# Graph layer on one Trainium2 core: a comparison moved to ScalarE, four comparisons merged into one, six node units moved into hop 2, output steps begun at tick 33

## The reference

```python
h = relu(layernorm(x))
agg = segment_sum(relu(h[src]), dst)            # layer 0
x = x + relu(relu((h + agg) @ W1 + b1) @ W2 + b2)
h = relu(layernorm(x))                          # layer 1, 8 heads of 8
Q = relu(h @ Wq + bq); K = h @ Wk + bk; V = h @ Wv + bv
hidden = V * hopwise[0]
for hop in range(3):
    if hop == 0:
        Kj = relu(K[row] + ef)
        msg = norm * outer(Kj, V[row]);  M = segment_sum(msg, col)
    else:
        M = segment_sum(norm * M[row], col)
    H = einsum("nhi,nhij->nhj", Q, M)
    H = H / max(1, |H| / sqrt(8))
    hidden += hopwise[hop + 1] * H
x = x + hidden
```

## Time and profile before

| | us |
|---|---|
| median of 3 runs | 1729.83 (1729.37 to 1741.05) |
| the profiled execution | 1737.73, its span 1735.0 |
| source pass, gathers | 3.7 to 285 |
| destination pass, gathers | 286 to 594 |
| hop 0, gathers | 640 to 895 |
| hop 1, gathers | 933 to 1190 |
| hop 2, gathers | 1211 to 1471 |
| scatters of the output | 1472 to 1725 |

### The profile page before, as it was taken

One profiled execution on the slowest core, in us unless ns is written; L12 is line 12 of the kernel. 1 busy time (PEld: TensorE's weight loads), 2 busy tenths in 40 slices (PEclk: granted clock), 3 DMA queues, 4 the chain that ended last, 5 costly groups with the idle time before them and its releaser, 6 DMA issues. The chain is left out here.

```text
span 1735.0 us, 22194 instructions
## 1 busy us (share of the span) xinstructions
PE 1301.4 (75%) x5794; PEld 800.3 (46%) x5794; DVE 1487.6 (86%) x3207; ACT 1017.0 (59%) x2815; POOL 1203.7 (69%) x1185
## 2 busy tenths in 40 slices
PE   3788888878888858777771777776588999777771
PEld 2666666656555534554550333323233444454551
DVE  5999999979999958999997999996456788799991
ACT  4688887858999954554552455553455666333330
POOL 7777766707777517777744777774777777777776
PEclk9799999979999967988895899899799999988886
DMA  5255554425666547999995788886345545466640
GB/s 130 80 115 114 127 123 113 127 70 147 159 170 157 145 93 249 317 320 314 305 313 183 271 308 305 300 307 242 92 124 155 158 135 154 132 177 173 176 138 16
DMA packets 281219, 313.83 MB, mean 181 GB/s; under 512 B 169009, under 2 KB 198569, under 8 KB 268550
## 3 DMA queue, kind: packets, MB, share of 16 engines
q1 hardware_dynamic: 224166, 246.39, 45.8%
q0 software_dynamic: 56928, 66.04, 15.0%
HBM read 214.54 MB, written 161.32 MB: 217 GB/s over the span
## 5 line engine op out<-in xcount | busy, mean ns | idle before, releaser
L946 PE MATMUL bank<-product,ident 128*128 128x512 f32 (+1 forms) x800 | 382.5, 635 | 137.6 <-DVE product L1302 137.5
L549 POOL DMA_INDIRECT state<-state_hop,slot_of_src x392 | 395.2, 1008 | 126.1 <-issue 108.0
L719 ACT ACTIVATE bank<-state,norm 128x512 f32<-128x512 f32 x392 | 251.2, 679 | 254.2 <-DMA state<-state_hop,slot_of_src 218.0
L1302 DVE TENSOR_TENSOR product<-bank,queries 128x512 f32<-128x512 f32 x392 | 261.9, 689 | 91.3 <-ACT bank L719 89.6
L946 PEld LDWEIGHTS bank<-product,ident 128*128 128x128 f32 x800 | 160.6, 206 | 357.7 <-issue 183.7
L511 POOL DMA_INDIRECT x_edges<-in_x,dst_tiles x196 | 203.5, 1039 | 106.2 <-issue 53.9
L525 POOL DMA_INDIRECT row_of_src<-node_rows,pos_int x196 | 195.3, 996 | 104.1 <-issue 54.3
L511 POOL DMA_INDIRECT x_edges<-in_x,src_tiles x196 | 210.0, 1071 | 75.1 <-issue 55.2
L565 POOL DMA_INDIRECT out<-rows,dst_out x196 | 193.3, 986 | 59.7 <-issue 58.8
L1300 DVE SCALAR_TENSOR_TENSOR acc<-acc,same_as_before,bank 128x512 f32<-128x512 f32 x196 | 145.7, 744 | 15.1 <-ACT bank L719 14.7
L1113 DVE SCALAR_TENSOR_TENSOR acc<-acc,same_as_before,bank 128x512 f32<-128x512 f32 x196 | 145.8, 744 | 1.7
(11 more groups left out here) (220 smaller groups left out, 2992.1 us busy)
## 6 DMA issues: line engine op xcount, KB each, us to landing
state_hop<-acc SPq DMA_DIRECT2D x98, 1024.0 KB, 4.6
x_nodes<-in_x SPq DMA_DIRECT2D x49, 256.0 KB, 4.2
src_row<-in_src_row SPq DMA_DIRECT2D x49, 256.0 KB, 3.9
out<-out_rows SPq DMA_DIRECT2D x49, 256.0 KB
dst_row<-in_dst_row SPq DMA_DIRECT2D x49, 256.0 KB, 3.4
kv_rows<-kv SPq DMA_DIRECT2D x49, 256.0 KB, 3.1
gg<-head_sums SPq DMA_DIRECT2D x98, 128.0 KB
kv_back<-kv_rows SPq DMA_DIRECT2D x49, 256.0 KB
```

The lines of the kernel that those rows point to most:

```text
L549: pool.indirect_dma_start(out=mg[u % 4][:, k, :], out_offset=None, in_=d_m[hop - 1], in_offset=bass.IndirectOffsetOnAxis(ap=sidx[:, t:t + ...
L719: act.activation(pw[t % len(pw)][:, :], mg[u % 4][:, k, :], ACT.Copy, scale=wn12[:, t:t + 1]).then_inc(weighted, 1)
L946: ins = ten.matmul(ph[:, 0:k * D].rearrange("p (c j) -> p c j", j=HD), ident[:, :], part, start=(r == 0), stop=(r == HD - 1))
L1302: vec.tensor_tensor(ihj(pr[m % 2][:, u % 2 * EH + k, :]), ihj(pw[t % len(pw)][:, :]), over_j(Q[:, t, :]), ALU.mult).then_inc(multiplied, 1)
```

## The change

1. `gsel` is made by ScalarE: Sign of `src_row` minus the first destination plus a half (1 or -1), at the end of its tick. `delta` is halved, its last column and the first row are set so that the product gives the same count; for this one more load (15 instead of 14) and three small VectorE operations stand before the first tick.
2. The four 128x128 comparisons of a unit become one 128x512 comparison with a broadcast column, behind the statistics.
3. The last six node units leave ticks 82 to 97 and run at E0+4, E0+8, ... E0+24. There the third product shares bank 0 with the two turns (`value_bank`), so TensorE waits before a turn until the sum of the older unit has been read; SP's first load of them waits for hop 1's states.
4. The head sums of hop 2 come one tick later in TensorE's queue.
5. The output steps in hop 2 begin at the first fitting tick from E0+33 (E0+34) instead of E0+10. So three full steps (f = 0, 1, 2) instead of eleven come before tick E0+50, and the last step is at E0+100 instead of E0+92.

```diff
-for g in range(E0 + 10, E0 + 3 * CU):
+for g in range(E0 + 33, E0 + 3 * CU):
...
-DENSE_TICKS = DENSE_TICKS[0:DU]
+DE = DU - 6
+DENSE_TICKS = DENSE_TICKS[0:DE] + [E0 + 4 + 4 * k for k in range(DU - DE)]
...
+        rowb = sb("row_begins", [P, 1])
...
+        def value_bank(m):
+
+            return pvd if m < DE else ptd
...
-        N_LOADS = 14
+        N_LOADS = 15
...
                 wait(sync, x1_d, m - RX + 1)
+                if m == DE:
+                    sync.wait_ge(carried, 2)
+                    for b in range(3):
+                        sync.wait_ge(m1_kept[b], landed(CU - 1, b, 3))
...
+                u = g - 1
+                if 0 <= u < CU:
+                    if u == 0:
+                        act.wait_ge(consts_set, 1)
+                    act.wait_ge(srow_in[u % 3], landed(u, u % 3, 3))
+                    wait(act, searched, u - 1)
+                    act.activation(gsel[u % 2][:, :], srow[u % 3][:, :], ACT.Sign, bias=rowb[:, 0:1]).then_inc(g_set, 1)
...
-                    rows_out(pvd, hT2d, Wv, 1, HT // 2, mm3_d)
+                    rows_out(value_bank(m), hT2d, Wv, 1, HT // 2, mm3_d)
...
+                    if m >= DE:
+                        wait(ten, res_d, len([t for t in DENSE_TICKS if t + 7 <= g]))
...
-                    m = group_ready(u) if 0 <= u < CU else None
+                    v = u if hop == 1 else u - 1
+                    m = group_ready(v) if 0 <= v < CU else None
...
+            step(vec.tensor_scalar(dprev[0:1, :], dprev[0:1, :], -1.0, None, ALU.mult))
             step(vec.tensor_tensor(delta[:, 0:T], dpm[:, :], dprev[:, :], ALU.subtract))
+            own.add(vec.tensor_scalar(delta[:, 0:T], delta[:, 0:T], 0.5, None, ALU.mult))
+            own.add(vec.tensor_scalar(rowb[:, :], dpm[:, 0:1], -1.0, 0.5, ALU.mult, ALU.add))
...
-                            ins = vec.tensor_scalar(sel[u % 2][:, k * P:(k + 1) * P], drow[u % 3][:, k * P:(k + 1) * P],
-                                                    tmf[:, t:t + 1], None, ALU.is_equal)
...
-                u = g - 1
-                if 0 <= u < CU:
-                    vec.wait_ge(srow_in[u % 3], landed(u, u % 3, 3))
-                    wait(vec, searched, u - 1)
-                    vec.tensor_scalar(gsel[u % 2][:, :], srow[u % 3][:, :], dpm[:, 0:1], None, ALU.is_ge).then_inc(g_set, 1)
+                u = g - S0
+                if 0 <= u < AU:
+                    vec.wait_ge(drow_in[u % 3], landed(u, u % 3, 3))
+                    wait(vec, turned_e, u - 1)
+                    vec.tensor_tensor(sel[u % 2][:, :].rearrange("p (k c) -> p k c", c=P),
+                                      drow[u % 3][:, :].rearrange("p (k c) -> p k c", c=P),
+                                      tmf[:, u * EH:(u + 1) * EH].unsqueeze(2).to_broadcast([P, EH, P]),
+                                      ALU.is_equal).then_inc(s_set, 1)
```

More of the change, by code:

```diff
@@ L397, in _ @@
             for to, what in ((dpm[:, :], dst_pm), (dprev[1:P, :], dst_pm[0:P - 1, :]),
+                             (dprev[0:1, :], dst_pm[P - 1:P, :]),
                              (brow[:, :], biases.unsqueeze(0).to_broadcast([3, 4 * P])),
@@ L942, in _ @@
                         if hop == 2 and m == 0:
-                            ten.wait_ge(res_d, DU)
+                            ten.wait_ge(res_d, DE)
                         for r in range(HD):
@@ L1080, in _ @@
             own.add(vec.memset(ones3[:, :], 1.0))
-            own.add(vec.memset(dprev[0:1, :], 0.0))
-            own.add(vec.memset(delta[:, T:T + 1], float(T)))
+            step(vec.memset(delta[:, T:T + 1], T / 2))
+            own.add(vec.memset(delta[0:1, T:T + 1], T + (P - 1) * T / 2))
             own.sync()
@@ L1121, in _ @@
                 qp, q = st[(g - 1) % RS], st[g % RS]
-                n_sel = 0
-                def select(n):
-                    nonlocal n_sel
-                    u = g - S0
-                    if 0 <= u < AU:
-                        if n_sel == 0:
-                            vec.wait_ge(drow_in[u % 3], landed(u, u % 3, 3))
-                            wait(vec, turned_e, u - 1)
-                        for k in range(n_sel, n_sel + n):
-                            t = u * EH + k
-                            ins = vec.tensor_scalar(sel[u % 2][:, k * P:(k + 1) * P], drow[u % 3][:, k * P:(k + 1) * P],
-                                                    tmf[:, t:t + 1], None, ALU.is_equal)
-                        n_sel += n
-                        if n_sel == EH:
-                            ins.then_inc(s_set, 1)
                 if g - 1 in STAT_NO:
@@ L1143, in _ @@
                     own.add(vec.reciprocal(qp[:, 4, lo:hi], qp[:, 3, lo:hi]))
-                    select(1)
                     own.sync()
@@ L1153, in _ @@
                     wait(vec, out_kept[m % 2], landed(m - 2, m % 2, 2))
-                    vec.tensor_tensor(flat(rd[m % 2][:, :, :]), pvd[:, :], flat(x1d[m % R1][:, 0, :, :]), ALU.add).then_inc(res_d, 1)
+                    vec.tensor_tensor(flat(rd[m % 2][:, :, :]), value_bank(m)[:, :], flat(x1d[m % R1][:, 0, :, :]), ALU.add).then_inc(res_d, 1)
                 m = DENSE_AT.get(g - 4)
@@ L1234, in _ @@
                         vec.wait_ge(x1_kept[b], landed(AU - 1, b, 4))
-                    vec.wait_ge(res_d, DU)
+                    vec.wait_ge(res_d, DE)
                     own.add(vec.memset(accz[2][:, EH - 1, :], 0.0))
```

5 lines of the change are left out of this document (removed).

## The result

| | before | after |
|---|---|---|
| time, median (lowest to highest) | 1734.1 us (1729.4 to 1741.1) | 1809.4 us (1803.9 to 1813.5) |
| ratio, with its 95% interval | | 1.043 (1.038 to 1.048) |
| span of the profiled execution | 1735.0 us | 1811.6 us |
| granted clock of TensorE | 0.890 | 0.864 |

The account below looks back on a forecast made before the run. From 1211 us to the end one GpSimd queue was taken as the bound, and its gathers before. Terms +1 - 0.5 + 0 - 12 + 23 + 18 = +29.5 us on 1729.8 gave 1759 us, range 1736 to 1773.

Parts of the forecast that it names:

- -0.5 us forecast: Source pass: the comparison leaving VectorE ran inside a wait for ScalarE's root, so 0.01 us x 48 ticks comes off.
- the slack just named also covers this: Source pass: ScalarE's 0.97 us idle per tick also absorbs TensorE's later search and the signs waiting for it; no cost.
- ScalarE late: Rival, source pass: Sign comes 0.3 us late in each of 48 ticks, +14 us, 1773 us; chance 0.08.
- the zero for the gathers: Destination pass: the wide comparison costs VectorE +12 us of time, but 0 (-3 to +4) us reaches the gathers.
- gathers get faster: Rival, destination pass: if narrow VectorE comparisons slow the gathers, 156 gathers gain 4 us, 1755 us; chance 0.08.
- -12 forecast: After the last destination gather: without six node units, tick 98 starts 4 us earlier and eight ticks save 8 us.
- two at 3.8, three at 3.0 and three at near 2 make 22 us: Eight ticks from tick 98: without node work they take 22 us instead of 29.9, -8 us.
- +23 forecast: Hop 2: node-unit rounds take 27.6 us against GpSimd's 20.8; products fall 34 us behind, buffers absorb 10.7, GpSimd held 23.
- The rival in which hop 2 takes the units in: Rival, hop 2: TensorE slips the matmul sets in, only some 4 us of the term stay, 1740 us; chance 0.28.
- +18 forecast: Tail: output begun at tick 33 makes scatters wait for rows, +18 us (16 to 26).
- 1496.7 + 47 x 5.1: Tail: second unit's row set at 1496.7 us, then 47 units at 5.1 us; last unit's first scatter at 1736.8.
- the 8 us that I took off for the head sums spread over two ticks: Tail: second unit set 8 us earlier, 1496.7 not 1504.69, with no output step in ticks 47 and 48 and head sums spread.

Follow-up runs that it names:

- the early Sign: Sign set ahead of ScalarE's wait for the search: in the kernel before (nothing else changed) 1729.9 us, ratio 0.995; in the changed kernel 1779.8 us, ratio 1.022.
- sign_early_wide: Kernel before with Sign ahead of ScalarE's wait for the search and the wide comparison; 1739.3 us, ratio 1.001.
- hop2_all_3: Kernel before with six node units moved into hop 2, its head sums one tick later and output from tick 33, comparisons unchanged; 1779.4 us, ratio 1.022.

## Why the forecast was wrong

**Sign, -0.5 us forecast, +20.0 measured.** The step that failed is "the slack just named also covers this". The 0.97 us a tick that ScalarE idles lie in front of its root, but Sign stands behind the root and both squares, and no idle time of ScalarE comes between. What counts is when TensorE wants the result: the earlier trace rows had VectorE's comparison done at 338.36, 0.6 us behind the last statistic's start; in the tick shown Sign ends 1.7 us behind the start of ScalarE's root (220.44 to 222.18) and so 1.95 us behind the last statistic's (220.23). The 14 us of the rival "ScalarE late" assumed 0.3 us a tick; it was the right rival, with a chance of 0.08, and too small a price: the pass lost 0.4 us a tick against the kernel before and 0.6 against the early Sign. It left out the lower clock, at which a quarter of the searches ran. What the forecast said of VectorE was right: the comparison ran inside a wait, and a plain tick gains 0.1 us.

**Wide comparison, 0 forecast, +7.** VectorE's own side was right: a wide one takes 0.688 us (0.68 forecast), and the last statistic and the reciprocal are 1.03 us apart (503.70 to 504.73; 1.0 forecast). What failed is the zero for the gathers: the forecast priced VectorE's time alone and set it against GpSimd's pace, and had the gathers' own time only the other way round, in the rival "gathers get faster". That rival falls: the 77 gathers of the kernel before that a narrow comparison overlaps took 1.000 us in the mean, none above 1.08, and with one wide comparison the mean of all rises from 1.039 to 1.043 us. In sign_early_wide the gathers' time is 5.4 of the 7 us, in the changed kernel 1.0 of 11.0, and the rest there is waiting; so the size of the term is shown and its cause only in part. The rest of the 11.0 us is company: the early Sign alone has 2 to 3 us more here than the kernel before, and the late one 2.9 us more than the early one (320.7 against 317.8), each no more than the rows repeat to.

The Trainium skill (SBUF — State Buffer, "Who interferes with whom" and the section on the two sides) says that GpSimd is shut out by a VectorE operation in a two-port mode, and by one with two SBUF inputs if GpSimd reads SBUF. The means agree in direction: source gathers fall from 1.071 to 1.045 us when the 0.48 us comparison leaves VectorE, and gathers beside a pass with two inputs from SBUF take longer (1.075 us beside the wide comparison, 1.13 to 1.22 beside the normalising passes of sign_early_wide). A full exclusion they don't show: 31 of 40 gathers beside a wide comparison were not slower than 1.08 us.

**Units out of the destination pass, -12 forecast, -3.0 in the changed kernel, -6.2 in hop2_all_3.** The first part of the term came and the second didn't. From the last destination gather to the first statistics of tick 98 the kernel before takes 7.9 us, the changed kernel 4.2 (625.2 to 629.39) and hop2_all_3 3.4: the -4 us. But the eight ticks from there, 29.9 us before, take 30.6 us in the changed kernel and 28.4 in hop2_all_3, where the forecast had 22. Their windows, of the kernel before and of the changed one, and VectorE's main wait in each (us, times, longest):

```profile
602.14:632.08 29.94, 24.86 (x148) 17.11 (x144) 24.21 (x83) 23.94 (x69) 0.00 (x0) 0.84 0.46 107
```
```profile
DVE stats L1143 <- ACT stats L666: 3.3, 5, 2.0
```
```profile
629.39:659.96 30.57, 21.26 (x106) 14.28 (x105) 16.90 (x62) 21.78 (x67) 0.00 (x0) 0.69 0.34 75
```
```profile
DVE stats L1151 <- ACT stats L677: 12.4, 7, 3.4
```

VectorE has 7.3 us less to do and waits 9.1 us more for ScalarE's root; ScalarE in turn waits 7.5 us for TensorE's matmuls, 2.0 us before. So the step that failed is "two at 3.8, three at 3.0 and three at near 2 make 22 us": it prices these ticks by VectorE's work, and the turn between TensorE and ScalarE keeps them at 4.0 to 5.7 us each for the first five. The granted clock is 0.84, 0.69 and, in hop2_all_3, 0.80; that it makes the difference between the drains of these two kernels, 2 of whose 3 us lie in these ticks, was not tried.

**Hop 2, +23 forecast, +28.3.** The mechanism is right and the round too, 27.6 forecast and 27.0 to 29.5 measured. The number of rounds was mis-sized: five ran at full length, not four, and the products were 38 us late at tick 28, not 34. The rival in which hop 2 takes the units in, with a chance of 0.28, is refuted.

**Tail, +18 forecast, +22.5.** The first unit's row is set 20.2 us behind the last gather's start, unit 1 at 28.4 (26.1 forecast), unit 48 at 264.5 (266.2; the forecast's own figures, 1496.7 + 47 x 5.1, make 1736.4 and not 1736.8): the rows come about as forecast. But the last scatter starts 275.7 us behind the last gather where the forecast's sum puts it at 271: GpSimd begins 21.4 us late and then needs 5.2 us a unit, and makes up none of it, though rows come every 5.0 us. The term that was mis-sized is GpSimd's: it starts 20 us later than before, and its own pace of 5.2 us a unit then sets the end, not the rows. And the 8 us that I took off for the head sums spread over two ticks are in truth the later head sums' 6.4 us; with the later output alone the tail grows by 28.6.

## What to carry to other kernels

When an instruction moves to another engine, compare the times at which its result is wanted and at which it is there, and not the idle time of the engine that takes it: the same Sign costs 20 us at the end of a tick and saves 9 at its middle. Work put under another engine's stream is priced by the order of the queues that it shares, and that can be laid out in a row and added up, with every round counted. Work taken off an engine shortens a tick only if that engine sets the tick: VectorE lost 7 of its 24 us in the eight ticks behind the destination gathers, and they took no less time. A term taken as zero needs as much care as the large ones.

## What the runs showed of the hardware that was not expected

- On the lower clock level the search took 2.99 us and on the higher 1.57 to 1.62 us. An idle time of 2.66 us in front of it went with the lower in two traces, but one of 2.67 us with the higher.
- Indirect gathers of 0.997 us in the median took 1.075 us in the mean beside the two-input comparison of 512 columns, 1.13 to 1.22 us beside the two-input normalising passes of the same run, and 1.00 us beside single-input comparisons of 128 columns.
- The same kernel took 1735 to 1740 us on some chips and 2077 to 2120 us on others, and one chip had both within seven minutes (2079 and then 1739 us). The durations of single instructions were the same, and one and the same change cost 4.3% or 0.5%.
